# Edge pass of a two-layer graph network: means and variances of the first norm kept in PSUM, epsilon of the second norm added by GpSimd

## The reference

```
h = relu(layernorm(x))
x = x + HGT(h)        # typed attention over the edges, gelu of the sums, x Wa by node type,
                      # mixed with h, layernorm, times ln_g[type] plus ln_b[type]
h = relu(layernorm(x))
x = x + GCN2(h)       # two graph convolutions
```

## Time and profile before

| | |
|---|---|
| median of 3 runs | 2772.43 us (2771.65 to 2778.87) |
| profiled execution, its own time | 2774.48 us |
| profiled execution, its span | 2772.8 us |
| DVE busy over the span | 2019.8 us (73%) |
| PE busy | 1846.7 us (67%) |
| GpSimd busy | 1676.0 us (60%) |
| ScalarE busy | 1176.9 us (42%) |
| granted TensorE clock, mean | 0.785 of full |
| edge pass, 1507 to 1870 us (363 us): DVE busy | 337.1 us |
| the same stretch: PE, ACT, POOL busy | 313.2, 229.1, 218.4 us |
| the same stretch: granted clock | 0.94 |

### The profile page before, as it was taken

How to read it: one execution, slowest core, us unless ns; L and a number is a source line. 1 busy time by engine, 2 the same in 40 slices (tenths; PEclk the granted TensorE clock), 3 DMA queues, 4 the chain that set the end, 5 groups by cost and what they waited for, 6 DMA issues and landing times. The chain is left out here.

```text
span 2772.8 us, 48253 instructions
## 1 busy us (share of the span) xinstructions
PE 1846.7 (67%) x12706; PEld 1451.0 (52%) x12706; DVE 2019.8 (73%) x6947; ACT 1176.9 (42%) x3234; POOL 1676.0 (60%) x1763
## 2 busy tenths in 40 slices
PE   3640069999999999999935888883555533333333
PEld 0110059999999999999933555552444322222221
DVE  7999769999999999999967999994444433333333
ACT  0000047777777777777723666662222211111111
POOL 0005567777777777777613656564666567667666
PEclk9985579999999999999967999895555555555555
DMA  7007957777777767777613555553444422222221
GB/s 198 0 0 256 349 154 183 184 180 179 181 181 183 186 181 182 185 182 182 175 43 85 144 143 152 145 135 92 110 111 118 107 65 66 63 62 66 61 65 47
DMA packets 425001, 373.00 MB, mean 135 GB/s; under 512 B 47762, under 2 KB 379390, under 8 KB 421760
## 3 DMA queue, kind: packets, MB, share of 16 engines
q1 hardware_dynamic: 385584, 275.36, 36.9%
q0 software_dynamic: 31360, 64.76, 11.3%
q10 hardware_dynamic: 7806, 29.98, 2.7%
HBM read 226.63 MB, written 146.53 MB: 135 GB/s over the span
## 5 line engine op out<-in xcount | busy, mean ns | idle before, releaser
L1674 DVE TENSOR_TENSOR_SCAN conv_sT<-keep,conv_sT,conv_pT 128x128 f32<-128x128 bf16 x390 | 186.7, 479 | 488.4 <-DMA t<-conv_res 202.8
L1655 PE MATMUL conv_pm<-w,conv_sT 128*128 128x128 f32 x784 | 279.8, 460 | 378.1 <-DVE conv_res L1681 236.3
L792 POOL DMA_INDIRECT att_xsd<-xt,ends_i x392 | 390.2, 995 | 95.1 <-issue 94.9
L1655 PEld LDWEIGHTS conv_pm<-w,conv_sT 128*128 128x128 f32 x784 | 196.3, 310 | 471.8 <-issue 313.6
L973 PE MATMUL att_kvc<-att_hm,w_kv 128*128 128x128 f32 x2352 | 296.9, 276 | 0.0
L1086 DVE TENSOR_TENSOR att_kvm<-att_kvc,att_rel_in 128x1024 f32<-128x1024 f32 x196 | 240.1, 1225 | 63.5 <-PE att_kvc L986 62.3
L973 PEld LDWEIGHTS att_kvc<-att_hm,w_kv 128*128 128x128 f32 x2352 | 280.8, 193 | 0.0
L1634 ACT ACTIVATE conv_row<-conv_row,ats 128x128 f32<-128x128 f32 x196 | 78.7, 401 | 474.6 <-DMA conv_row<-t,idx 457.9
L1603 POOL DMA_INDIRECT out_dram<-conv_res,out_i x196 | 197.5, 1008 | 112.6 <-issue 99.9
L1649 PE MATMUL conv_pT<-ident,conv_row 128*128 128x128 f32 x392 | 168.0, 429 | 134.5 <-issue 109.0
L1597 POOL DMA_INDIRECT conv_row<-ta,idx x196 | 185.0, 944 | 105.1 <-issue 43.5
(11 more groups left out here) (240 smaller groups left out, 4817.7 us busy)
## 6 DMA issues: line engine op xcount, KB each, us to landing
att_mask_in_t<-type_row SPq DMA_DIRECT2D x196, 192.0 KB
xt<-xr ACTq DMA_DIRECT2D x23, 1224.0 KB
att_nxr<-xt SPq DMA_DIRECT2D x97, 262.0 KB
att_rel_in<-rel_row SPq DMA_DIRECT2D x196, 128.0 KB
out_dram<-att_not SPq DMA_DIRECT2D x97, 256.0 KB
ta<-att_nhs SPq DMA_DIRECT2D x97, 256.0 KB
xr<-in_x_dram SPq DMA_DIRECT2D x20, 1088.0 KB
xd_rows<-att_xsd SPq DMA_DIRECT2D x196, 65.5 KB
```

The lines of the kernel that those rows point to most:

```text
L792: pool.indirect_dma_start(out=xsd[:, v, k, :], out_offset=None, in_=xt, in_offset=bass.IndirectOffsetOnAxis(ap=ends_i[:, n, k:k + 1], axis ...
L1655: nc.tensor.matmul(pm[:, k % 2, 0:D], sT[:, k % R], w[:], start=True, stop=True).then_inc(m_ready, 1)
L1674: dve.tensor_tensor_scan(sT[:, n % R], keep[:, n * P:(n + 1) * P], pT[:, n % 2, 0:P], before, ALU.mult, ALU.add).then_inc(s_ready, 1)
```

## The change

Two things are changed. First, the tile `mv` of the first norm (mean and variance, two numbers for each of 7 tiles) no longer lies in SBUF but in the eighth, unused slot of the PSUM tile `pc` of the same group. So L1494 of the first norm writes PSUM, L1498 of the first norm reads PSUM, and L1545 reads its means from PSUM and `rstd` from SBUF. Second, variance plus epsilon of the second norm is no longer computed by DVE (L1498) but by GpSimd, right ahead of its power L1366, with a semaphore `ve2` between the two; `var2` now comes from the last L1494. The tile `mv` of the second norm stays in SBUF under the name `mv2`.

```diff
-            mv = [[lb(f"mv{k}{b}", [P, G, 2], F32) for b in two] for k in two]
+            mv2 = [lb(f"mv2{b}", [P, G, 2], F32) for b in two]
...
+            mv = [[pc[b][:, G, 0:2 * G].rearrange("p (j o) -> p j o", o=2) for b in two], [mv2[b][:] for b in two]]
...
                             pool.wait_ge(var2, g + 1)
                             if g >= 2:
                                 pool.wait_ge(nm2, g - 1)
+                            pool.tensor_scalar(ve[1][b][:], mv2[b][:, :, 1], EPS, None, ALU.add).then_inc(ve2, 1)
+                            pool.wait_ge(ve2, g + 1)
                             pool.tensor_tensor(rstd[1][b][:], ve[1][b][:], mh[:], ALU.pow).then_inc(rstd2, 1)
...
-                    def spreads(k, g, of, then):
+                    def spreads(k, g, of):
...
                         for j in range(G):
                             m = dve.bn_aggr(mv[k][g % 2][:, j], st[:, k, j])
+                        if k:
+                            m.then_inc(var2, 1)
+                            return
                         m.then_inc(small, 1)
                         n[0] += 1
                         dve.wait_ge(small, n[0])
-                        dve.tensor_scalar_add(ve[k][g % 2][:], mv[k][g % 2][:, :, 1], EPS).then_inc(then, 1)
+                        dve.tensor_scalar_add(ve[0][g % 2][:], mv[0][g % 2][:, :, 1], EPS).then_inc(var1, 1)
...
-                            spreads(0, g, pc[g % 2], var1)
+                            spreads(0, g, pc[g % 2])
...
-                            spreads(1, g, x1[g % 3], var2)
+                            spreads(1, g, x1[g % 3])
```

More of the change, by code:

```diff
@@ L1286, in hgt_then_graphconv @@
             pc_ready, pg_ready, pg_read = ls("pc_ready"), ls("pg_ready"), ls("pg_read")
-            st0_done, st1_done, var1, var2, rstd1, rstd2 = ls("st0_done"), ls("st1_done"), ls("var1"), ls("var2"), ls("rstd1"), ls("rstd2")
+            st0_done, st1_done, var1, var2, ve2, rstd1, rstd2 = ls("st0_done"), ls("st1_done"), ls("var1"), ls("var2"), ls("ve2"), ls("rstd1"), ls("rstd2")
             nm1, nm2, y_half, y_done, hs_done, x1_step, x1_done, small = (
```

## The result

The kernel after takes 2751.22 us (median of 6 runs, 2748.05 to 2755.53) against 2772.04 for the kernel before (6 runs, 2763.51 to 2778.87) on the same chip: 20.8 us less, ratio 0.9922, 95% interval 0.9908 to 0.9935. It is faster, by more than the 13.4 us of the forecast, and lies just at the low edge of the range of 2751 to 2771. The profiled execution took 2754.5 us with a span of 2752.8, 20.0 less than that of before.

The account below looks back on a forecast made before the run. DVE was taken to set the step, in a ring with GpSimd. 8.5 + 4.8 + 1.8 - 1.5 - 0.2 = 13.4 us gained, forecast 2759.1 us; own range 2753 to 2766, 8-in-10 range 2751 to 2771.

Parts of the forecast that it names:

- the slowed stretches of PE: Edge pass: five in 25 steps, each worth some 1.5 us more, two more or fewer; used only for the range.
- Part 1, the holding is only moved: DVE in short steps: L1545 freed, but L1512 behind it held until the first mask product ends; gain 1.8 us.
- Rival 1: L1512 passes the mask product, so the whole holding goes: 46.6 us gained, 2725.8; chance 0.08.
- The price of PSUM, 1.5 us: First norm's last L1494 writing and L1498 reading PSUM: 0.06 per step, 1.5 us lost; range 0 to 6.8.
- Part 2, the holding of 8.5 us: Second norm's L1498 on DVE, held in 10 long steps at 0.85 us each; all 8.5 us goes.
- Part 2, the plain cost: DVE between the second norm's L1494 and L1505, without L1498 and its wait: 0.19 per step, 4.8 us gained.
- The long steps: Steps with slowed PE: about 1 us shorter, PE's idle time ahead of its first group falling to about 0.4.
- Rival 2: PE becomes the bound in long steps; their ten gains of 1.05 are lost, 2.9 us stay: 2769.5; chance 0.12.
- Rival 3: GpSimd's later power holds L1512 of the first four tiles, 0.57 in 15 short steps, 8.6 us: 2767.7; chance 0.06.
- Rivals 4 and 5: Rival 4: L1512 stands through the second mask product too, 22.2 us slower, 2794.6; chance 0.06. Rival 5 has its own line.
- Rival 5: L1545 stays held despite PSUM, and PSUM costs 6.8 instead of 1.5: 8.1 us gained, 2764.3; chance 0.05.
- The two ends of the pass: Drained end of the pass: nothing covers GpSimd's added addition, 0.2 us lost once.

Follow-up runs that it names:

- e3: Kernel after with DVE's addition of three tiles moved ahead of L1481 and L1485, before GpSimd's mask product: 2707.86 us, ratio 0.9754 to the kernel before.
- e2: Second half alone: kernel after with mean and variance of both norms in SBUF; 2753.96 us, ratio 0.9924 to the kernel before.
- e1: First half alone: kernel before with mean and variance of the first norm in PSUM; 2771.59 us, ratio 0.9989 to the kernel before.
- the repeat: Kernels before and after, unchanged, traced once more on another chip: 2671.88 and 2650.99 us, one run each.
- b_again: Kernel before, unchanged, run once more on another chip for its trace: 2671.88 us.
- e7: Kernel before with only the order of e4 (both additions of x1 and xr moved), nothing of the change: 2771.13 us, ratio 0.9992 to the kernel before.
- a_again: Kernel after, unchanged, run once more on another chip for its trace: 2650.99 us.
- e5: Kernel after plus a wait and a spare one-input L1497-like instruction where the second norm's L1498 stood: 2658.48 us, ratio 0.9947 to the kernel before, other chip.
- e4: As e3, with the addition of four tiles also moved, behind the following L1481 and L1485: 2702.3 us, ratio 0.9734 to before; again 2701.87, 0.9744.
- e6: e4 with the first norm's mean and variance in SBUF: 2632.85 us, ratio 0.9853 to before, other chip; beside e4 2735.05 us, 0.986.

## Why the prediction was wrong

The mechanism of the first half held, and the sum was too small: the slowed stretches of PE were put down as scatter where they had a direction, and PSUM was charged with a price that it does not have.

- **Part 1, the holding is only moved**: right. The addition takes 2.50 us in a short step (about 2.4 was said) and ends with the first product. Rival 1, the whole holding gone, is out; e3 shows it was there to be had, behind that addition.
- **The price of PSUM, 1.5 us**: it was not there. L1497 takes 8 ns more, L1504 165 ns against 171 from SBUF (e2), and e1 gained the full 0.07 a step. The nearest row, a read of 128 columns, did not carry over to 2 or 7 numbers.
- **Part 2, the holding of 8.5 us**: right in size, 8.4 (ten steps), 10.0 in the repeat.
- **Part 2, the plain cost**: 0.23 a step, not 0.19; over 24 steps and not 25 that is 5.5 for 4.8.
- **The step that failed**: "stretches of slowed PE, five in these 25 steps, each worth some 1.5 us more once L1498 is out, of which two more or fewer may fall". I took their number as scatter with no direction and put it at nothing in the sum. Fully slowed starts numbered 3, 3, 4 and 5 within the 24 steps of the traces with a held L1498 (before, b_again, e1, e7) and 1, 2, 1, 1, 0, 0, 0 in those without (after, a_again, e2, e5, e3, e4, e6). Two fewer is 2.9 us here, one fewer 1.5 in the repeat. Together with the holding that is 11.3 us here and 11.5 in the repeat, where the sum had 8.5. I also priced the held L1498 at its own length; e2 and e5 show that without the holding a slowed step is not followed by a second one. That the holding raises the number of fully slowed starts is what the counts say; by what steps it does so is not shown.
- **The long steps**: they were to fall by about 1 us with PE's idle time at 0.4. Measured 0.26 to 0.35 idle, and 13.56 instead of 14.67, 15.0 instead of 16.23: 1.1 and 1.2. Rival 2, PE as the bound, is out.
- **Rival 3, the power holds the addition of four tiles**: out. L1518 at 1657.99 starts inside the power 1657.10 to 1658.61 and takes 0.69; held until 1658.61, it would have ended 0.5 us later than it did. The Trainium skill, "SBUF — State Buffer", section "Who interferes with whom", says that a DVE instruction with two SBUF inputs contends with a GpSimd instruction that reads SBUF. The trace agrees for the mask product (2.50 instead of 0.54) and not for the power.
- **Rivals 4 and 5**: out. No addition stood through both products (2.50, not over 4), and `nmr` takes 141 ns. Rival 5 was also added up wrongly: with `nmr` held as before, the 1.8 us of the first half would not come either, and 6.3 us would be left instead of 8.1.

In numbers, from the one pair of traces: 13.4 forecast; plain step 7.2 instead of 5.1 (4.8 + 1.8 - 1.5), fully slowed starts 2.9 instead of 0, holding 8.4 instead of 8.5. That makes 18.6 for the steps. The two ends of the pass gave 0.8 where 0.2 lost had been put down. The rest up to 20.8 is smaller than what runs of one kernel differ by.

Still open is why PE's clock falls where it does. The traces show only what goes with it: stretches at the lower level where PE idles 1.3 to 2.2 us ahead of its first group in a step of 12.9 to 13.9 us (1.3 in e6), and none between 1510 and 1790 us in e3 and e4, where it idles 0.3 or less in nearly every step. Nothing here varied that idle time alone.

## What to carry to other kernels

When an instruction is held, look at the next one in its queue: if that would be held by the same thing, freeing the first only passes the stall on, and order and buffer have to change together (alone the PSUM tile gave 3 us and the order 2; beside the second half, which gave 21 by itself, the order gave 17 more without the PSUM tile and 50 more with it). A small held instruction on the engine that sets the step can cost more than its own time (11.3 us against 8.4 here), so price an edit with the rows of the slowed steps as well as of the clean ones. And try the parts of a change in each other's presence before one is called worthless.

## What the runs showed of the hardware

A power on GpSimd does not hold DVE's addition, but the addition delays the power. The two in order of time in the kernel after:

```profile
1754.33 0.69 DVE L1518 TENSOR_TENSOR edge_x<-edge_x,edge_xr 128x512 f32<-128x512 f32 x1
1754.47 1.91 POOL L1369 TENSOR_TENSOR edge_rstd<-edge_ve,edge_mh 128x7 f32<-128x7 f32 x1
```

A power that starts 0.14 after the addition takes 1.91 instead of 1.51, while one that is under way when the addition starts (1657.10) takes its 1.51 and leaves the addition at 0.69. Likewise GpSimd's small addition took 0.69 instead of 0.24 beside DVE's in e3. DVE's small operations cost about as much with PSUM operands as with SBUF ones: L1497 162 against 154 ns written, L1504 165 against 171 (e2) read, and `nmr` with one PSUM input 141 against 167 for the second norm's `nmr`, all in SBUF.
